# One copy of the transposed probabilities on ScalarE, and two DMAs that ScalarE issues to lay them out

## What is computed

```python
def local_attention(q, k, v):        # 16 heads of 64, windows of 32 tokens
    bk2, bv2 = look(bk), look(bv)    # each window sees itself and the one before: 64 keys
    sim = einsum('bhwie,bhwje->bhwij', bq, bk2) * 8.0
    sim = where(mask, -max, sim)
    attn = softmax(sim, -1)
    return einsum('bhwij,bhwje->bhwie', attn, bv2)
...
for i in range(6):
    x = attn_layer(shift_tokens(x), ...) + x    # qkv, l2norm, rotary, local_attention, Wo
    x = ffn_layer(shift_tokens(x), ...) + x     # layer norm, W1, a * gelu(gate), W2
```

## Time and profile before

| | before |
|---|---|
| median of 3 runs | 1713.03 us (1712.72 to 1717.97) |
| the profiled execution | 1714.56 us, its span 1712.8 us |
| mean granted TensorE clock | 0.984 |
| busy: PE, DVE, ACT, POOL | 1589.8, 1465.7, 1417.6, 1311.1 us |
| chain that ended last | PE 46%, ACT 33%, issue 15%, DVE 4% |

### The profile page before, as it was taken

How to read it: one execution, slowest core, us unless ns; L and a number is a source line. 1 busy time by engine, 2 the same in 40 slices (tenths; PEclk the granted TensorE clock), 3 DMA queues, 4 the chain that set the end, 5 groups by cost and what they waited for, 6 DMA issues and landing times.

```text
span 1712.8 us, 68566 instructions
## 1 busy us (share of the span) xinstructions
PE 1589.8 (93%) x25874; PEld 1282.7 (75%) x25874; DVE 1465.7 (86%) x3011; ACT 1417.6 (83%) x2851; POOL 1311.1 (77%) x1305
## 2 busy tenths in 40 slices
PE   7879999999999999999999999999999999999995
PEld 5667777777777777777777777777777777777773
DVE  3499998998998898899889889988988988888874
ACT  3267988888888888888888888888888888888885
POOL 6088877878887787888778778877877877777765
PEclk8899999999999999999999999999999999999997
DMA  4011111111111111111111111111111101110000
GB/s 152 31 38 44 35 33 37 33 47 41 39 32 31 37 43 36 49 31 32 31 39 46 43 37 31 32 32 52 40 35 37 31 28 44 34 32 26 28 24 26
DMA packets 41426, 66.40 MB, mean 39 GB/s; under 512 B 7072, under 2 KB 16032, under 8 KB 41376
## 3 DMA queue, kind: packets, MB, share of 16 engines
q1 hardware_dynamic: 40224, 65.38, 12.7%
q10 hardware_dynamic: 1152, 0.34, 0.1%
HBM read 20.61 MB, written 1.05 MB: 13 GB/s over the span
## 4 chain that ended last, share of the span: by engine, by line
PE 46%; ACT 33%; issue 15%; DVE 4%; ACTq 1%; DMA 0%; POOL 0%; DVEq 0%; POOLq 0%
PE ps_qs L530 11%; PE ps_q L530 8%; PE ps_a L530 6%; PE ps_po L530 6%; PE ps_tk L530 5%; ACT squares L949 4%; ACT q_t L943 4%; ACT prob L987 4%; ACT p_bd L943 4%; ACT L1053 3%; ACT L1050 3%; ACT ps_qs L943 3%; PE ps_f L530 3%; PE ps_v L530 2%; PE ps_k L530 2%
## 5 line engine op out<-in xcount | busy, mean ns | idle before, releaser
L419 POOL TENSOR_TENSOR qk<-qk,qk_rot 128x512 f32<-128x512 f32 x384 | 483.8, 1282 | 0.0
L427 POOL TENSOR_TENSOR qk<-qk,rnorm 128x512 f32<-128x512 f32 x384 | 393.4, 1046 | 68.2 <-DVE rnorm L1284 63.7
L434 POOL TENSOR_TENSOR prob<-prob,row_inv 128x512 f32<-128x512 f32 x192 | 200.6, 1045 | 133.4 <-DVE row_inv L1301 133.2
L530 PE MATMUL ps_qs<-k_t,q_t 64*32 64x64 f32 x12224 | 209.7, 217 | 60.9 <-ACT ps_qs L943 60.8
L1264 DVE TENSOR_REDUCE ssq<-squares 128x8 f32<-128x512 f32 x384 | 260.7, 679 | 3.4 <-ACT squares L949 3.4
L530 PEld LDWEIGHTS ps_qs<-k_t,q_t 64*32 64x32 f32 x12224 | 181.3, 107 | 76.5 <-issue 67.0
L943 ACT COPY attn_t<-ps_po 128x512 f32<-128x512 f32 x191 | 113.3, 593 | 131.0 <-PE ps_po L530 130.9
L943 ACT COPY p_bd<-ps_po 64x512 f32<-64x512 f32 x378 | 217.8, 576 | 2.4 <-PE ps_po L650 0.2
L530 PEld LDWEIGHTS ps_po<-p_bd,v_back 128*64 128x64 f32 x3056 | 166.9, 137 | 37.5 <-issue 17.2
L530 PE MATMUL ps_po<-p_bd,v_back 128*64 128x64 f32 x3056 | 190.9, 223 | 0.0
L530 PE MATMUL ps_po<-p_bd,v_own 128*64 128x64 f32 x3056 | 188.7, 222 | 0.0
(11 more groups left out here) (237 smaller groups left out, 4095.5 us busy)
## 6 DMA issues: line engine op xcount, KB each, us to landing
v_back<-v_own SPq DMA_DIRECT2D x192, 192.0 KB, 2.4
w_raw<-in_wqkv SPq DMA_DIRECT2D x48, 192.0 KB, 2.4
v_back<-v_own SPq DMA_DIRECT2D x96, 64.0 KB, 2.1
wo_sb<-in_wo SPq DMA_DIRECT2D x12, 256.0 KB, 2.9
w_sb<-in_w SPq DMA_DIRECT2D x6, 341.0 KB, 3.2
w_sb<-in_w SPq DMA_DIRECT2D x6, 192.0 KB, 2.7
x_in<-in_x SPq DMA_DIRECT2D x4, 256.0 KB, 4.1
out<-s_out SPq DMA_DIRECT2D x8, 128.0 KB, 1.9
```

The lines of the kernel that those rows point to most:

```text
L419: nc.gpsimd.tensor_tensor(qk[:, s, i, :], qk[:, s, i, :], qk_rot[:, s, i, :], ALU.add).then_inc(added, 1)
L427: nc.gpsimd.tensor_tensor(heads(qk[:, s, i, :]), heads(qk[:, s, i, :]), rnorm[:, s, 8 * i:8 * i + 8].unsqueeze(2).to_broadcast([P, 8, HEAD ...
L434: nc.gpsimd.tensor_tensor(heads(prob[:, s, :]), heads(prob[:, s, :]), row_inv[:, s, :].unsqueeze(2).to_broadcast([P, 8, HEAD]), ALU.mult). ...
L530: return nc.tensor.matmul(o, lhs, rhs, start=start, stop=stop, **kw)
```

## The change

The core of the diff:

```diff
         prob = sb("prob", [P, 2, OCTET])
-        p_bd = sb("p_bd", [P, 2, PAIRS * 4, 2, WINDOW])
+        p_t = sb("p_t", [P, 2, OCTET])
+        p_bd = sb("p_bd", [P, 2, 2, OCTET])
...
+        p_placed = [sem(f"p_placed_{s}") for s in range(2)]
...
-            def values(u, n, j, s, ps=ps_po):
-
-                pe.wait_ge(p_turned, u + 1)
+            def values(u, n, j, s, ps=ps_po, placed=False):
+
+                if placed:
+                    pe.wait_ge(p_placed[s], (2 * n + j // 2 + 1) * 32)
+                else:
+                    pe.wait_ge(p_turned, u + 1)
                 pe.wait_ge(v_shifted[j], (n + 1) * (32 if j % 2 else 16))
...
-                                      p_bd[:, s, 4 * c + 2 * odd + head].rearrange("p a b -> p (a b)"), True, True,
+                                      p_bd[:, s, :, span(WINDOW * (4 * c + 2 * odd + head), WINDOW)], True, True,
...
-            def keep_p(u, s, ps=ps_po):
+            def keep_p(u, s):
+
                 wait(act, o_done, u - 1)
+                act.wait_ge(pt_done, u + 1)
+                copy(p_t[:, s, :], ps_po[:]).then_inc(p_turned, 1)
+
+            def place_p(u, s):
+
+                act.wait_ge(p_turned, u + 1)
+                for h in range(2):
+                    rows = slice(64 * h, 64 * h + 64)
+                    act.dma_start(p_bd[rows, s, h, :], p_t[rows, s, :]).then_inc(p_placed[s], 16)
...
                     if live(u - 3):
                         softmax_exp(u - 3, (j - 3) % 2)
+                    if live(u - 4):
+                        place_p(u - 4, j % 2)
                     squares_of(u, 1, j % 2)
```

More of the change, by code:

```diff
@@ L819, in body @@
                     if live(u - 4):
-                        values(u - 4, n - 1, j, j % 2)
+                        values(u - 4, n - 1, j, j % 2, placed=True)
             def drain():
@@ L975, in keep_turned_k, with keep_p_halves @@
                      ps[:].rearrange("p (c t) -> p c t", t=P)).then_inc(k_turned, 1)
-            def keep_p(u, s, ps=ps_po):
+            def keep_p(u, s):
                 wait(act, o_done, u - 1)
+                act.wait_ge(pt_done, u + 1)
[5 more added lines that the diff above has]
+                    act.dma_start(p_bd[rows, s, h, :], p_t[rows, s, :]).then_inc(p_placed[s], 16)
+            def keep_p_halves(u, s, ps=ps_po):
+                act.wait_ge(o_done, u - 1)
                 act.wait_ge(pt_done, u + 1)
@@ L981, in keep_p @@
                     rows = slice(64 * h, 64 * h + 64)
-                    last = copy(p_bd[rows, s, :, h, :], ps[rows, :].rearrange("p (g q) -> p g q", q=WINDOW))
+                    last = copy(p_bd[rows, s, h, :], ps[rows, :])
                 last.then_inc(p_turned, 1)
@@ L1090, in drain @@
                 start_norms(d, 1)
-                keep_p(a, 0)
+                keep_p_halves(a, 0)
                 keep_turned_q(c, 0, ps_q)
@@ L1098, in drain @@
                 softmax_exp(c, 0)
-                keep_p(b, 1, ps_tk)
+                keep_p_halves(b, 1, ps_tk)
                 ln_square(LAST - 1)
@@ L1105, in drain @@
                 start_norms(END, 1)
-                keep_p(c, 0, ps_v)
+                keep_p_halves(c, 0, ps_v)
                 load_gelu()
                 gelu(LAST - 3)
-                keep_p(d, 1, ps_k)
+                keep_p_halves(d, 1, ps_k)
                 keep_attention(c, LAST, 2, ps_tk)
```

## The result

The changed kernel takes 1752.13 us (median of 4 runs, 1751.28 to 1753.3), the kernel before 1714.58 (median of 4, 1712.72 to 1717.97). The ratio is 1.0217 (95% interval 1.0197 to 1.0237), so the change costs 37.5 us. The forecast was 1734, which is 21 us more, with a range up to 1758. The profiled execution took 1751.28 us, its span is 1749.5.

What follows compares the result with a forecast made beforehand. ScalarE was taken to bound the second slot and TensorE the fourth. A 0.52 us delay less two 0.03 us gains gave 0.46 us a pass, 21 us in 45 passes: 1734 us, range 1702 to 1758.

Steps and rivals of the forecast that it cites:

- One copy of 590 ns in each slot, ScalarE busy 107 us less: Expected profile sign on ScalarE: one copy of about 590 ns per slot, busy time about 107 us less in 188 slots.
- Two DMA rows of 0.51 each, the squares of k 1.81 us behind the copy: ScalarE's queue: two issues take 1.05 us with 0.03 between; squares of k start 1.81 us after the copy's start, against 1.84.
- the term g: ScalarE's gain per slot, saved copy less uncovered issue time: 0.03 us, counted twice a pass against 0.52 us lost.
- the rival: ScalarE's DMA issue doesn't hold what is behind it: g 0.57, -0.62 us a pass, -28 us, 1685 us; chance 0.08.
- Landing 2.2 to 2.3 us after the issue: DMAs into p_bd: 128 KB lands 2.25 us after its issue starts, 2.79 us from the copy's end to the second landing.
- A wait for a DMA in the second slot only, about 1.8 us: TensorE idles some 1.8 us ahead of the second slot's values; no wait for the mask, none for DMAs in other slots.
- The first slot's cover of 0.49 us: First slot: output projection matmuls hide the landing with 0.49 us to spare, values ready at 894.16 against their start at 894.65.
- A pass of 33.66: One loop pass was to take 33.66 us, against 33.2 before: 0.46 us more.
- the issue is dear: Rival: each ScalarE issue takes 0.59 us, g is -0.13, a pass gains 0.86 us, 39 in all, 1752 us; chance 0.12.
- The term of 0.57 saved: ScalarE, each slot: one 0.59 us copy replaces two taking 1.16 us, saving 0.57 us if nothing else came.
- TensorE is full in the fourth slot, so nothing there takes the 0.52 us back: The second slot's scores start 0.52 us later; TensorE, busy throughout the fourth slot, can't recover that delay.
- three written-out passes: Passes outside the loop counted with its 42, making 45 at 0.46 us each; earlier ones, without gelu or feed-forward, counted nothing.

Runs made afterwards that it cites:

- issue_alone: Kernel before with p_bd's new layout and its two copies; ScalarE also issues two dummy DMAs behind its exponential, which the values don't await: 1834.31 us, ratio 1.0706.
- sp_issues: Changed kernel with its two DMAs issued by SyncE instead of ScalarE: 1697.88 us, ratio 0.9914 to the kernel before.
- warm: Changed kernel with 12 extra 128x128 matmuls on TensorE ahead of the values in the second slot: 1793.09 us, ratio 1.0457 to the kernel before.
- warm_half: Changed kernel with 6 extra 128x128 matmuls on TensorE ahead of the values in the second slot: 1755.72 us, ratio 1.0257 to the kernel before.
- landing_alone: Kernel before with p_bd's new layout and its two copies; SyncE issues two dummy DMAs behind them, and the values wait for these: 1790.3 us, ratio 1.0449.
- both_issue: Changed kernel with one DMA issued by ScalarE and the other by SyncE at the same time: 1701.82 us, ratio 0.9924 to the kernel before.

## Why the prediction was right, and where it was short

The sign and the mechanism held, step by step:
1. *One copy of 590 ns in each slot, ScalarE busy 107 us less.* 581 ns, and 123 us less.
2. *Two DMA rows of 0.51 each, the squares of k 1.81 us behind the copy.* The pair takes 1.12 and not 1.05: the first 0.49, the second then 0.61. The restart takes 0.16 in most slots and 0.24 in the first, against 0.17. So the squares of k are 1.89 behind the copy, 1.97 in the first slot, against 1.84 before: ScalarE loses 0.05 and 0.13 us where the term g had a gain of 0.03. As the prediction expected, and as the Trainium skill's page Perfetto Trace Analysis (DMA Instruction, HWDGE) has it, what is behind the DMAs starts only when their issue has ended. The experiment issue_alone shows it: with nothing waiting for these DMAs, the squares of k moved from 1.84 to 2.55 us behind the copies. This contradicts the use that I made of the Trainium skill's page Advanced Engine Details and Errata (Sequencer Loop) for the rival.
3. *Landing 2.2 to 2.3 us after the issue.* 2.39. TensorE then started after 0.12 and not 0.25. From the copy to the values it is 3.62 us, against 0.59 + 2.79 + 0.25 = 3.63: two errors that cancel.
4. *A wait for a DMA in the second slot only, about 1.8 us.* 1.85 in the second slot. The first slot's cover of 0.49 us held in 34 of the 42 passes. It failed in the five whose first slot is 8.6 to 8.8, and by 0.3 to 0.4 us in three others (8.1 to 8.2); the second slot is then shorter by about as much, so this cost little. The prediction had named it as a sign of being wrong.
5. *A pass of 33.66.* 33.96 in a regular one.

**The regular pass: the mis-sized term is g.** The prediction has 0.46 us a pass, and 0.75 was measured. The second slot was forecast at 8.75 and is 8.94. Its copy starts 4.24 us into the slot, where 4.11 less a gain of 0.03 was forecast; 0.16 of the 0.19 us is this, ScalarE's loss in the first slot arriving in the second. Another 0.04 lies between values and scores (1.08 against 1.04). In the third slot, `ff_down` starts 6.47 us in, and 6.42 before; with the gain of 0.03 that was forecast, this makes up the 0.07 by which the slot is longer than forecast (8.85 against 8.78). The rest is 0.03 in the other two slots. 0.29 x 42 = 12 us of the shortfall come from there. The pass lies between the forecast's 0.46 and the 0.86 of the rival *the issue is dear*, whose g of -0.13 is that of the first slot.

**The term of 0.57 saved was mis-sized too, and hidden.** With the issue moved away (sp_issues), the squares of k are 1.00 us behind the copy and not 1.84. Going from two copies to one was thus worth 0.84 us, and the issue cost ScalarE 0.89. The sum came out near the forecast as both were larger by about as much.

**What no step had: the clock.** The prediction ends with *TensorE is full in the fourth slot, so nothing there takes the 0.52 us back*, and prices the idle time of 1.8 us at its own length. In five passes it cost 1.35 us more each, 6.8 us in all. That the gap lets the clock fall is supported by warm and warm_half, where no pass of the loop lost it, by sp_issues, whose shorter gap never did, and by issue_alone and landing_alone, whose longer gaps did so more often. What picks the five of 42 is open.

**What was counted as nothing: the passes ahead.** The forecast has 0.46 us each for three written-out passes, 1.4 us, and nothing for the earliest. Of the 3.0 us measured ahead of the loop, 2.3 are in the second and third pass (n = 1 and 2), which the forecast left out, and 0.7 in the two behind them; the last written-out pass cost nothing.

19.3 us for 42 passes, 12 for g and the slots, 6.8 for the clock and 1 for the five passes with a late first slot make the loop's 39, and the passes ahead add 3.0. The spans differ by 5.7 us less, because of the two stretches that the change doesn't touch. With these as long as before, the total would be 1752.1 + 5.7, about 1758 by my estimate, at the upper end of the range; that it came out lower is luck.

**Why the change is slower, in short.** With the two halves apart: the landing alone adds 1.23 us a pass (landing_alone), the issue alone 2.2 (issue_alone), and taking away a copy pays only part of it back. With the issue on SyncE the saved copy outweighs the landing (-0.51 us a pass, sp_issues). With it on ScalarE the saving is gone and what is left is the second slot with its landing: 0.68 of the 0.75 us. One DMA for both halves, each half with another offset, wasn't tried.

## What to carry to other kernels

A DMA that a computing engine issues is work on that engine: count here 0.5 to 0.6 us each plus a restart of about 0.2, from the moment its wait is released, and subtract only what the instruction ahead still runs. If a queue is there that no one waits for, issue from it; here this alone turned 2.2% slower into 0.9% faster, and starting the chain earlier in the one slot where the landing shows made it 2% faster (1681 us). Price a new landing slot by slot against its cover, and treat a gap in front of a busy TensorE as more than its own length until a trace shows that the clock holds.

## What the runs showed of the hardware that I had not expected

- Of two DMAs issued back to back from one queue the second holds the sequencer longer: 0.49 and 0.61 us on ScalarE for 64 x 512 f32.
- Two DMAs issued at the same time from two queues (both_issue) landed after 2.4 and 2.9 us, so the later one was no sooner in place than from one queue.
- One copy of 128 partitions lets the next activation start 0.46 us after its own start (894.21 to 894.67), though it is shown as 0.58 long. A pair of 64 partitions each lets it start after 1.18 us (919.20 to 920.38 in issue_alone). Replacing the pair by one saves more than the rows' lengths say.
- Equal gaps had unequal results: after about 1.85 us of idle time TensorE's granted clock fell to 0.52 in 5 of 42 passes. After about 2.2 us (landing_alone) it fell in 12 of 42, after 2.13 us (issue_alone) in 29 of 42, and after 1.13 us (sp_issues) or 1.18 us (before) in none.
